# One step of attention, another order of TensorE's score halves, logits and mixes

## The chip, the core and the metric

The kernel runs on one core of a Trainium2 chip. The metric is the device time of the whole program in microseconds (us): 3871.87 is the median of three runs of the kernel before (3871.11 to 3872.05).

TensorE (PE) does the matrix products, VectorE (DVE) and ScalarE (ACT) read its results out of PSUM, GpSimd (POOL) adds in SBUF and issues the accumulating transfers, SyncE (SP) issues the plain ones. Each engine runs its own instructions strictly in the order in which the program lists them, and waits on semaphores that the others raise.

## What is computed

Cross-attention with grouped queries: 4 batches, 1024 queries, 1601 keys, 32 heads of 32, 8 key/value heads (4 query heads share one), then an output projection, a residual and a layer norm, all in float32.

```python
q = hidden_state @ Wq + bq;  k = encoder_hidden_state @ Wk + bk;  v = encoder_hidden_state @ Wv + bv
scores = jnp.einsum('bkgld,bksd->bkgls', q, k) * scale + encoder_attention_mask[:, :, None, :, :]
attn = jax.nn.softmax(scores, axis=-1)
out = jnp.einsum('bkgls,bksd->bkgld', attn, v)
x = out.transpose(0, 3, 1, 2, 4).reshape(b, l, H) @ Wo + bo + hidden_state
return (x - mean(x)) * rsqrt(var(x) + EPS) * gamma + beta
```

The mask of these inputs is zero everywhere. The kernel tests that on the chip and takes a branch without mask work.

## The kernel before

Three stages follow each other. `project` makes q, k and v and writes them to DRAM. `attend` does the attention, and it is all that the change touches. `output` does the projection and the norm.

`attend` runs 64 steps: a step is 512 queries of one batch with one key/value head and its 4 query heads. Steps are written out in groups of four (`QUAD`). Work of one step, by the letters of the string `ORDER` (line 475):

- **S**, a score half (line 821): two matmuls over half of the 1601 keys into one of the two `score` buffers, for 128 queries of one head. VectorE then takes the maximum over them (line 972). There are 32 in a step, for the step after this one. After the last of a step, VectorE joins the halves to `row_max` (line 976).
- **T**, once: the row maxima of the next step are transposed into a `logit` bank (line 852). ScalarE and VectorE split them into two parts `parts_t` (lines 1036, 984), and SyncE copies these as two more rows under that step's queries (`shift`, line 632), so that the logits come out with the maximum taken off.
- **L**, a logit tile (line 866): 128 keys by 512 queries of one head, one matmul into one of three `logit` banks. ScalarE takes the exponential into `weights` (line 1030). There are 52 in a step: 13 key tiles (0 to 12) of 4 heads.
- **M**, a mix (line 876, from `mix`): weights times values for one key tile. Four heads side by side, each 32 columns of the array. It needs the four exponentials of its tile. There are 13 in a step; the first of a step's string is tile 12 of the step before (`FIRST_MIX = 1`).
- **P**, once: the sums over the keys (`denominators`, line 876 too) of the step before, from `sum_pool`.

The order of TensorE's work is this string, read from left to right in every step; ScalarE follows the same string, and VectorE follows the sequence of the S. Between the letters stand the waits. An S waits until VectorE has read the score half two before it. L, T and P take the three `logit` banks in turn, so each waits for the reader of the third before it. A mix waits for its exponentials.

GpSimd adds the weights of 9 of the 13 tiles into `sum_pool` by 8 adds (line 736). The other four (2, 5, 8, 11) are added by accumulating transfers that it issues (three at line 747; `merge` at line 754 adds their sum to `sum_pool` after the first add of the next step, once the third has landed). ScalarE may overwrite a weights buffer only when its mix and its add are done: the exponentials of tile 4, the 17th to 20th L of a step, take the buffer of tile 12 of the step before, whose add is GpSimd's eighth.

SyncE's own order within a step: the queries and keys of a later step (`load_step`, lines 603 and 606, once the 52nd L of the step is done), their values (lines 610 and 611, once the step's last mix is done), the store of the mixed rows, the store of the sums (line 645, after P and its copy), and then the shift rows (line 632).

Of the kernel before, what the change touches and what calls it, by code (L numbers as in the profile page):

```python
# [53 lines left out]
def xattn_program(nc, x, ctx_kv, mask, wq, bq, wk, bk, wv, bv, wo, bo, gamma, beta, out):  # L54
    x_flat = x.rearrange("b l h -> (b l) h")
    ctx_flat = ctx_kv.rearrange("b s h -> (b s) h")
    mask_flat = mask.rearrange("b o l s -> (b o l) s")
    out_flat = out.rearrange("b l h -> (b l) h")

    q_dram = nc.dram_tensor("q_parts", [NLQ, KVH, 2, P, LQ], F32, kind="Internal").ap()  # L60
    k_dram = nc.dram_tensor("k_parts", [2, KV, B * S], F32, kind="Internal").ap()
    v_dram = nc.dram_tensor("v_rows", [B * S, KV], F32, kind="Internal").ap()
    a_dram = nc.dram_tensor("weighted", [NSTEP, P, LQ], F32, kind="Internal").ap()
    d_dram = nc.dram_tensor("denominators", [NSTEP, G, LQ], F32, kind="Internal").ap()
    r_dram = nc.dram_tensor("reciprocals", [NSTEP, G, LQ], F32, kind="Internal").ap()
    wo_dram = nc.dram_tensor("wo_parts", [2 * KVH, P, H], F32, kind="Internal").ap()

    with ExitStack() as whole:
        ident = whole.enter_context(nc.sbuf_tensor("ident", [P, P], F32))
        mask_size = whole.enter_context(nc.sbuf_tensor("mask_size", [P, MT], F32))  # L70
        project(nc, x_flat, ctx_flat, mask_flat, wq, bq, wk, bk, wv, bv, wo, q_dram, k_dram, v_dram, wo_dram, ident, mask_size)

        qk_store = [whole.enter_context(nc.sbuf_tensor(f"qk_store{i}", [P, G * LQ + S], F32R)) for i in range(3)]
        wo_spare = whole.enter_context(nc.sbuf_tensor("wo_spare", [P, H], F32R))
        wo_in = whole.enter_context(nc.semaphore("wo_parts_in"))
        wo_slots = [store[:, t * H:(t + 1) * H] for store in qk_store for t in range(SLOTS)] + [wo_spare[:]]
        attend(nc, mask_flat, q_dram, k_dram, v_dram, a_dram, d_dram, r_dram, wo_dram, ident, mask_size, qk_store, wo_spare, wo_in)
        output(nc, x_flat, wo_slots, wo_in, wo_dram, bo, gamma, beta, a_dram, d_dram, r_dram, out_flat)
# [384 lines left out]
def attend(nc, mask_flat, q_dram, k_dram, v_dram, a_dram, d_dram, r_dram, wo_dram, ident, mask_size, qk_store, wo_spare, wo_in):  # L463
# [8 lines left out]
    LATE = 10  # L472
    NPOOL = len(POOL) - 1

    ORDER = "LLLSLSLLSLMSLLSLMMSLLSLLSLSLLSLMMSLLSLLSLSLLSLMMSLLSLLSLSLLSLPMMLSLSLLLSLSTMMLLSLLSLSLLSLSLLSLMMSLS"
    FIRST_MIX = 1
    LO_AT = 24
    assert [ORDER.count(k) for k in "LSMTP"] == [ST * G, 2 * NROW, ST, 1, 1]
    BANKS = 3
    USES = [k for k in ORDER if k in "LTP"]  # L480
    assert len(USES) % BANKS == 0
# [40 lines left out]
    with ExitStack() as held:  # L522
# [278 lines left out]
        def _(pe):  # L801
# [105 lines left out]
            def quad_steps(quad, masked, first=False, last=False):  # L907
                for s in range(QUAD):
                    u = k = 0
                    tile = s * ST - FIRST_MIX  # L910
                    for work in ORDER:
                        if work == "L":
# [96 lines left out]
        def _(act):  # L1009
# [40 lines left out]
            def quad_steps(quad, first=False, last=False):  # L1050
                for s in range(QUAD):
                    u = mixes = 0
                    for work in ORDER:
                        if work == "L":
# [259 lines left out]
```

## Time and profile before

| | |
|---|---|
| time, median of three runs | 3871.87 us |
| the profiled execution: its own time | 3873.77 us |
| its span | 3872.1 us |
| TensorE busy | 3769.2 us (97%) |
| TensorE weight loads busy | 2379.7 us (61%) |
| VectorE busy | 2496.9 us (64%) |
| ScalarE busy | 2033.2 us (53%) |
| GpSimd busy | 2895.5 us (75%) |
| attention, from the first P to the 62nd | 900.09 to 3415.97 us |
| TensorE's granted clock from 900 to 3416 us | 1.00 |

Times count from the start of the span. In the busy time of TensorE the matmuls overlap each other: the next one starts before the last has ended. So the distance between two starts tells more than the durations. A mix appears as 8 matmuls, so "x16" is two mixes and "x12" is one and a half, where a window cuts; a score half appears as "x2", a logit tile as "x1".

### The profile page before, as it was taken

Reading aid. Unit: us, or ns where it says so; the run is one execution under the profiler, and the core shown is the slowest. Engines: PE = TensorE matmul, PEld = TensorE weight load, DVE = VectorE, ACT = ScalarE, POOL = GpSimd, SP = SyncE. Lnnn points to the kernel's source line nnn. Section 1 sums busy time; section 2 is a strip of 40 time slices with the busy share of each in tenths; the row PEclk is TensorE's granted clock in tenths of the full one; section 3 lists DMA queues with packets and bytes.
Section 4 is the critical chain, followed back from the end, with each engine's and each line's share of the span. In section 5 each row is a group of like instructions: output and inputs, shape, how many; then the busy total and the mean of one; then the engine's idle time right before and its main releaser. Section 6 shows DMA issues by size and latency. Waiting matters only on the chain. (4 is left out here: it accounts for less than half of the span.)

```text
span 3872.1 us, 55400 instructions
## 1 busy us (share of the span) xinstructions
PE 3769.2 (97%) x20306; PEld 2379.7 (61%) x20306; DVE 2496.9 (64%) x2904; ACT 2033.2 (53%) x3854; POOL 2895.5 (75%) x1104
## 2 busy tenths in 40 slices
PE   8999999789999999999999999999999999988998
PEld 7998888545555555555555555555555555536886
DVE  3334444477777777777777777777777777725665
ACT  2222112126666666666666666676666666661110
POOL 1111111139999999999999999999999999984555
PEclk9999999869999999999999999999999999998999
DMA  5344555647667667667667667677677677667664
GB/s 176 136 150 177 201 198 200 246 85 152 146 146 155 145 145 158 143 145 159 146 144 158 145 146 158 141 151 155 139 155 151 141 155 149 146 150 220 194 191 125
DMA packets 294100, 611.94 MB, mean 158 GB/s; under 512 B 131696, under 2 KB 168688, under 8 KB 261360
## 3 DMA queue, kind: packets, MB, share of 16 engines
q0 software_dynamic: 58080, 337.15, 38.7%
q1 hardware_dynamic: 232528, 265.54, 25.7%
q10 hardware_dynamic: 3264, 6.29, 0.5%
q8 instruction: 134, 2.20, 0.2%
q14 instruction: 94, 0.77, 0.1%
HBM read 244.50 MB, written 96.99 MB: 88 GB/s over the span
## 5 line engine op out<-in xcount | busy, mean ns | idle before, releaser
L972 DVE TENSOR_REDUCE half_max<-score 128x1 f32<-128x800 f32 (+1 forms) x2048 | 1893.7, 986 | 714.2 <-PE score L821 710.2
L1030 ACT ACTIVATE weights<-logit 128x512 f32<-128x512 f32 (+1 forms) x3328 | 1732.4, 602 | 791.6 <-PE logit L866 765.6
L736 POOL TENSOR_TENSOR sum_pool<-sum_pool,weights 128x2048 f32<-128x2048 f32 x446 | 2125.6, 4766 | 29.6 <-ACT weights L1030 2.5
L821 PE MATMUL score<-qk_store 96*128 96x400 f32 (+1 forms) x4096 | 1212.2, 378 | 14.9 <-DMA qk_store<-k_parts 10.4
L866 PE MATMUL logit<-qk_store 98*128 98x512 f32 (+1 forms) x3328 | 1199.5, 417 | 2.3 <-ACT weights L1030 2.2
L821 PEld LDWEIGHTS score<-qk_store 96*128 96x128 f32 x4096 | 688.5, 191 | 552.6 <-DVE half_max L972 397.5
L876 PE MATMUL mixed<-weights,v_sb 128*32 128x512 f32 x6656 | 807.8, 599 | 0.7 <-ACT weights L1030 0.7
L866 PEld LDWEIGHTS logit<-qk_store 98*128 98x128 f32 (+1 forms) x3328 | 607.8, 185 | 264.0 <-ACT weights L1030 135.1
L876 PEld LDWEIGHTS mixed<-weights,v_sb 128*32 128x32 f32 x6656 | 177.0, 109 | 393.2 <-ACT weights L1030 218.6
L736 POOL TENSOR_TENSOR sum_pool<-weights 128x2048 f32<-128x2048 f32 x64 | 313.7, 4901 | 63.6 <-ACT weights L1030 63.6
L450 POOL DMA_DIRECT2D q_parts<-o_hi x64 | 34.5, 540 | 306.1 <-DVE o_lo L412 149.3
L1192 PE MATMUL acc<-qk_store,a_hi 128*128 128x512 f32 x576 | 187.0, 397 | 25.1 <-DVE a_lo L1227 25.1
L347 ACT ACTIVATE o_hi<-summed,bq_scaled 128x512 fp32r<-128x512 f32 x64 | 44.1, 689 | 304.0 <-PE summed L259 274.3
L325 ACT CAST t_hi<-turned 128x512 fp32r<-128x512 f32 x168 | 95.6, 585 | 141.8 <-PE turned L254 141.8
L407 DVE TENSOR_SCALAR full<-summed,bq_scaled 128x512 f32<-128x512 f32 x64 | 48.0, 751 | 188.5 <-ACT o_hi L347 188.5
L747 POOL DMA_DIRECT2D weights<-weights x191 | 165.9, 868 | 0.0
L1281 POOL TENSOR_TENSOR total<-total,beta_row 128x1024 f32<-128x1024 f32 x32 | 100.4, 3139 | 76.3 <-DVE total L1248 76.3
L1274 POOL TENSOR_TENSOR total<-total,bo_row 128x1024 f32<-128x1024 f32 x32 | 89.6, 2806 | 85.4 <-DMA total<-in_x 85.2
L456 POOL DMA_DIRECT2D v_rows<-v_store x52 | 28.1, 540 | 160.1 <-DMA v_rows<-v_store 101.5
L1192 PEld LDWEIGHTS acc<-qk_store,a_hi 128*128 128x128 f32 x576 | 109.4, 190 | 52.6 <-issue 26.0
L372 DVE TENSOR_TENSOR t_lo<-turned,t_hi 128x512 fp32r<-128x512 f32 x168 | 113.1, 685 | 42.6 <-ACT t_hi L325 42.4
L259 PE MATMUL summed<-t_hi,wq_hi 128*128 128x512 f32 x512 | 134.6, 404 | 0.0
(87 smaller groups left out, 2772.4 us busy)
## 6 DMA issues: line engine op xcount, KB each, us to landing
weights<-weights POOLq DMA_DIRECT2D x191, 1024.0 KB, 7.3
sum_pool<-weights POOLq DMA_DIRECT2D x63, 1024.0 KB, 7.0
qk_store<-q_parts SPq DMA_DIRECT2D x192, 256.0 KB, 3.9
qk_store<-k_parts SPq DMA_DIRECT2D x192, 200.1 KB, 5.4
rows<-in_ctx SPq DMA_DIRECT2D x26, 1024.0 KB, 5.1
landing<-in_mask_Bx1xSxS_ff SPq DMA_DIRECT2D x32, 800.5 KB, 5.5
rows<-in_x SPq DMA_DIRECT2D x16, 1024.0 KB, 5.1
q_parts<-o_hi POOLq DMA_DIRECT2D x64, 256.0 KB, 2.4
```

The costliest lines, as they stand in the source:

```text
L259: last = nc.tensor.matmul(acc, lhs, rhs, start=(n == 0), stop=(n == len(pairs) - 1))
L325: nc.scalar.copy(t_hi[par][:, t, :], turned[t % 2][:]).then_inc(hi_done, 1)
L372: nc.vector.tensor_tensor(t_lo[par][:, t, :], turned[t % 2][:], t_hi[par][:, t, :].bitcast(F32), ALU.subtract).then_inc(lo_done, 1)
L736: nc.gpsimd.tensor_tensor(sum_pool[s % 2][0:w], first[0:w], weights[buffer(s, st)][0:w], ALU.add).then_inc(pool_added, 1)
L747: pool.dma_start(weights[buffer(s, REST[0])][:], weights[buffer(s, st)][:], accum_op=ALU.add).then_inc(rest_added, 16)
L821: last = nc.tensor.matmul(score[j][:, c, 0:w], q_sb[buf][0:STACK, h, lt * P:(lt + 1) * P], k_sb[buf][0:STACK, start:start + w], start=True ...
L866: last = nc.tensor.matmul(bank[0:w, :], k_sb[s][:, keys], q_sb[s][:, h, :], start=True, stop=not masked, skip_group_check=masked)
L876: last = nc.tensor.matmul(out[h * HD:(h + 1) * HD, :], lhs, rhs[0:w, h, :], start=start, stop=stop)
L972: nc.vector.tensor_reduce(half_max[m // NROW % 2][:, k % G, k // G, j:j + 1], score[j][:, :, 0:HALVES[j][2]], mybir.AxisListType.XY, ALU.m ...
L1030: nc.scalar.activation(weights[buffer(s, st)][0:w, h, :], logit[u % BANKS][0:w, :], ACT.Exp).then_inc(exp_done, 1)
L1192: last = nc.tensor.matmul(acc[j * NT + t][:, n, :], a[:, k, cols], w[k][:, out_cols], start=(k == 0 and m == 0), stop=(k == KVH - 1 and m ...
L1281: nc.gpsimd.tensor_tensor(total[r][:], total[r][:], beta_row[:], ALU.add).then_inc(final, 1)
```

## The change

One string is another. It has the same letters in the same numbers, 52 L, 32 S, 13 M, one T, one P, and all else is as it was.

```diff
@@ -472,7 +472,7 @@
     LATE = 10
     NPOOL = len(POOL) - 1
 
-    ORDER = "LLLSLSLLSLMSLLSLMMSLLSLLSLSLLSLMMSLLSLLSLSLLSLMMSLLSLLSLSLLSLPMMLSLSLLLSLSTMMLLSLLSLSLLSLSLLSLMMSLS"
+    ORDER = "LLMSLLSLLSLLSLSLLSLLSLLSLLSLLSLSLLLSLSMMMMSLLSLLSLLSLSLLSLLSLLSLMLTSLSMMMSLSMMPLSLLSLLSLLSLLSLMMSLS"
     FIRST_MIX = 1
     LO_AT = 24
```

A visit is a run of M and P without anything else between. Before there are seven in a step: M, MM, MM, MM, PMM, MM, MM. Now there are six: M, MMMM, M, MMM, MMP, MM.

TensorE, before, inside the branch without mask, from one pair of mixes to the P (score is an S, logit an L, the second operand `weights,v_sb` a mix):

```order
L876 MATMUL mixed<-weights,v_sb 32x512 x8
L821 MATMUL score<-qk_store 128x402 x2
L866 MATMUL logit<-qk_store 128x512 x2
L821 MATMUL score<-qk_store 128x400 x2
L866 MATMUL logit<-qk_store 128x512 x2
L821 MATMUL score<-qk_store 128x402 x2
L866 MATMUL logit<-qk_store 128x512
L821 MATMUL score<-qk_store 128x400 x2
L866 MATMUL logit<-qk_store 128x512 x2
L821 MATMUL score<-qk_store 128x402 x2
L866 MATMUL logit<-qk_store 128x512
L876 MATMUL logit<-sum_pool,ones 32x512 x4
```

The pair of mixes is 8 instructions here. Five S and eight L stand between two visits, and an L is the last of them.

TensorE now, the end of the longest run and what follows it:

```order
L866 MATMUL logit<-qk_store 128x512 x2
L821 MATMUL score<-qk_store 128x402 x2
L866 MATMUL logit<-qk_store 128x512
L821 MATMUL score<-qk_store 128x400 x2
L866 MATMUL logit<-qk_store 128x512 x3
L821 MATMUL score<-qk_store 128x402 x2
L866 MATMUL logit<-qk_store 128x512
L821 MATMUL score<-qk_store 128x400 x2
L876 MATMUL mixed<-weights,v_sb 32x512 x16
L821 MATMUL score<-qk_store 128x402 x2
```

Four mixes (16 instructions) stand together, and the last thing before them is an S. The run before them holds 13 S and 22 L.

TensorE now, from the third visit to the P:

```order
L876 MATMUL mixed<-weights,v_sb 32x512 x4
L866 MATMUL logit<-qk_store 128x512
L852 MATMUL logit<-ident,row_max 16x128
L821 MATMUL score<-qk_store 128x402 x2
L866 MATMUL logit<-qk_store 128x512
L821 MATMUL score<-qk_store 128x400 x2
L876 MATMUL mixed<-weights,v_sb 32x512 x12
L821 MATMUL score<-qk_store 128x402 x2
L866 MATMUL logit<-qk_store 128x512
L821 MATMUL score<-qk_store 128x400 x2
L876 MATMUL mixed<-weights,v_sb 32x512 x8
L876 MATMUL logit<-sum_pool,ones 32x512 x4
```

The transpose T stood after the P before (35th L, then 41st); now it comes first, after 39 L, and the P comes after 41. ScalarE's copies of both move with them.

## Rows read from the trace of the kernel before

**Rows 1.** The page's groups: busy time, mean ns, idle before, releaser

```profile
L972 DVE TENSOR_REDUCE half_max<-score 128x1 f32<-128x800 f32 (+1 forms) x2048 | 1893.7, 986 | 714.2 <-PE score L821 710.2
L1030 ACT ACTIVATE weights<-logit 128x512 f32<-128x512 f32 (+1 forms) x3328 | 1732.4, 602 | 791.6 <-PE logit L866 765.6
```

**Rows 2.** TensorE in order of time, one step: start, duration, instruction, count

```profile
1989.08 0.98 PE L866 MATMUL logit<-qk_store 98*128 98x512 f32 x3
...
1992.32 1.07 PE L876 MATMUL mixed<-weights,v_sb 65*32 65x512 f32 x8
1993.32 0.63 PE L821 MATMUL score<-qk_store 96*128 96x402 f32 x2
...
1994.96 1.92 PE L876 MATMUL mixed<-weights,v_sb 128*32 128x512 f32 x16
...
2007.29 1.92 PE L876 MATMUL mixed<-weights,v_sb 128*32 128x512 f32 x16
2009.15 0.64 PE L821 MATMUL score<-qk_store 96*128 96x402 f32 x2
2009.63 0.62 PE L866 MATMUL logit<-qk_store 98*128 98x512 f32 x2
2010.09 0.53 PE L821 MATMUL score<-qk_store 96*128 96x400 f32 x2
2010.45 0.76 PE L866 MATMUL logit<-qk_store 98*128 98x512 f32 x2
...
2013.16 0.39 PE L866 MATMUL logit<-qk_store 98*128 98x512 f32 x1
2013.48 1.06 PE L876 MATMUL logit<-sum_pool,ones 128*32 128x512 f32 x8
...
2019.71 1.92 PE L876 MATMUL mixed<-weights,v_sb 128*32 128x512 f32 x16
...
2027.38 1.92 PE L876 MATMUL mixed<-weights,v_sb 128*32 128x512 f32 x16
...
2033.54 1.06 PE L876 MATMUL mixed<-weights,v_sb 65*32 65x512 f32 x8
```

**Rows 3.** The same view, the 62nd P

```profile
3415.97 1.06 PE L876 MATMUL logit<-sum_pool,ones 128*32 128x512 f32 x8
```

**Rows 4.** VectorE in order of time; in brackets its idle time before

```profile
2003.65 4.59 DVE L972 TENSOR_REDUCE half_max<-score 128x1 f32<-128x800 f32 x5 [1.57 <-PE score L821]
```

**Rows 5.** ScalarE in order of time, in that burst and in the last step

```profile
2003.88 4.21 ACT L1030 ACTIVATE weights<-logit 128x512 f32<-128x512 f32 x8 [1.97 <-PE logit L866]
...
3439.18 4.03 ACT L1030 ACTIVATE weights<-logit 128x512 f32<-128x512 f32 x8 [1.08 <-PE logit L866]
```

**Rows 6.** GpSimd in order of time, one cycle of it

```profile
1992.67 4.89 POOL L736 TENSOR_TENSOR sum_pool<-sum_pool,weights 65x2048 f32<-65x2048 f32 x1
...
2002.55 0.87 POOL L754 DMA_DIRECT2D sum_pool<-weights  x1 [0.44 <-POOL sum_pool L736]
...
2033.05 0.87 POOL L747 DMA_DIRECT2D weights<-weights  x1
2033.64 4.88 POOL L736 TENSOR_TENSOR sum_pool<-sum_pool,weights 65x2048 f32<-65x2048 f32 x1
2038.16 4.91 POOL L736 TENSOR_TENSOR sum_pool<-weights 128x2048 f32<-128x2048 f32 x1
2043.33 0.87 POOL L754 DMA_DIRECT2D sum_pool<-weights  x1 [0.26 <-POOL sum_pool L736]
```

**Rows 7.** SyncE's transfers in order of time

```profile
2015.43 0.63 SPq L645 DMA_DIRECT2D denominators<-denom_sb  x1
2021.06 1.17 SPq L632 DMA_DIRECT2D qk_store<-parts_t  x2
2030.34 1.34 SPq L603 DMA_DIRECT2D qk_store<-q_parts  x3
```

**Rows 8.** From the view of the tile parts_t: landing of the shift rows' transfers

```profile
DMA to landing us min/median/max: 1.8/1.8/5.6
```

## The prediction

> **What bounds the kernel now.** First the page's groups [rows 1]: VectorE's maxima wait 710 us in all for a score, ScalarE's exponentials 766 us for a logit. Neither reader is the bound over the whole. Next, TensorE in order of time: 900.09 (first P; in the table of times) and 3415.97 [rows 3] are 61 steps apart, 41.24 us each, and the step in [rows 2] (1992.32 to 2033.54) has 41.22. TensorE never stands long, so the question is what its slots hold. From [rows 2] by distances of starts:
>
> - an S takes 0.36 (2010.09 to 2010.45), which I take as 0.365, two L 0.46 (2009.63 to 2010.09), so 0.235 each;
> - a visit with one mix occupies 1.00 (1992.32 to 1993.32), one with two 1.86 (2007.29 to 2009.15): a mix is 0.857, and leaving costs 0.115 to 0.14. The first S behind a visit takes 0.48 instead of 0.365: 0.115 more. The last L before one takes 0.32 (2013.16 to 2013.48): 0.09 more. A visit thus costs 0.32 beside its mixes.
>
> A step's slots are 52 x 0.235 + 32 x 0.365 + 14 x 0.857 + 0.20 for T = 36.1, and seven visits add 2.3. The remaining 2.8 of 41.24 are waits inside the runs between visits. [Rows 4] show whose: in a run VectorE takes five halves in 4.59 back to back, each complete after 0.986 [rows 1], so one per (4.59 - 0.99) / 4 = 0.90 (0.901 unrounded); then it idles 1.57 while TensorE mixes. An S needs the half two before it read, so within a run TensorE goes at VectorE's pace, and in a visit VectorE starves, because only what stands in two score buffers is left for it. ScalarE's pace is read from the last step, which has no S and where it is the limit: eight exponentials in 4.03 [rows 5], one complete after 0.60 [rows 1], so one per (4.03 - 0.60) / 7 = 0.49.
>
> **The change part by part.** Nothing is computed more or less; only runs and visits are cut differently. I write a step as its mixes, 14 x 0.857 = 12.0, plus the runs between visits.
>
> Before, from [rows 2], each run being a visit's start less the start and mixes of the visit before: 1.78 (2 S, 3 L), two of 4.45, 4.48 behind 2009.00 (each 5 S, 8 L), 3.66 (4 S, 6 L, T; 2016.05 to 2019.71), 5.96 (6 S, 11 L; 2021.42 to 2027.38), 4.45 (5 S, 8 L). Together 29.2; with the mixes 41.2, as measured.
>
> The rule for a run: it begins with 0.23 of leaving and refilling; VectorE begins 0.20 behind the first S's slot; after that S number n can start only 0.06 after half n-2 has been read, plus 0.115 because its weights were not loaded ahead; then its own slot, a trailing L, and 0.09 for entering. For n = 5: 0.23 + 0.365 + 0.20 + 2 x 0.90 + 0.99 + 0.17 + 0.365 + 0.235 + 0.09 = 4.45, which is the measured run.
>
> Now, by the same rule, run by run:
> - 13 S and 22 L, ending in an S: 0.23 + 0.565 + 10 x 0.901 + 1.155 + 0.365 + 0.09 = 11.42 (1.155 is 0.985 + 0.17). ScalarE has 22 x 0.49 = 10.8 beside it and little room where three L stand together; I add 0.14: 11.56.
> - 8 S, 14 L: 0.23 + 0.565 + 5 x 0.901 + 1.155 + 0.60 + 0.09 = 7.15; with 0.07 for ScalarE 7.22.
> - L T S L S: slots and a visit's cost, 1.70. S L S: 1.30.
> - 5 S, 10 L behind the P: here ScalarE is slower, 10 x 0.49 against 5 x 0.90: 4.91.
> - S L S and the two L of the next step: 1.76, as the 1.78 before.
> Sum 28.45, and with the mixes 40.45. The same walk gives 41.15 for the step before, 0.09 under the trace, so I put 40.54. Where the 0.7 comes from: 0.3 is the visit less; 0.4 is that three runs now end in an S directly before the visit, so VectorE has up to two halves to read when a visit begins, and starves less often. The longest visit costs it nothing more per mix.
>
> The Trainium skill, TensorEngine Tiling (Array Packing), Key Properties, says that a change of tiling mode drains TensorE. Counted by that rule alone the change is worth one drain in a step, 0.3 x 62 = 20 us; [rows 4] say that more than half of the gain is VectorE's, which that rule doesn't hold.
>
> What the trace doesn't show is a visit entered directly from an S (three times now). The nearest rows are an L before it (0.09 more than its slot) and the next score behind an S without any cost; I take 0.09, with 0 and 0.19 as ends: 3 x 62 x -0.09 to 3 x 62 x +0.10, or -17 to +19 us.
>
> **GpSimd.** Its cycle from one merge's issue to the next is 2043.33 - 2002.55 = 40.78 [rows 6], nearly the step. Without a wait it would be 2038.16 - 2002.55 = 35.61 and one add of 4.52 (2038.16 - 2033.64), together 40.13. The rest is the wait of the merge for the third accumulating transfer, issued 2033.05, merge 2043.33: 10.3 us for one that otherwise lands in 7. It collides with the query and key loads, which SyncE issues at 2030.34 [rows 7], behind the 52nd L. These are tied to TensorE's step, and so GpSimd follows it. A step of 40.54 is 0.4 above GpSimd's 40.13, so it can follow, with less room. One place gets tight: the 17th L now ends 8.9 us behind the step's first instead of 11.3 (slots and runs as above), and its exponential overwrites the buffer whose add is GpSimd's last. That add starts at 1992.67 and ends at 1997.56, 8.5 behind the step's first L (1989.08). In a step shorter by 0.6 it ends at 9.1, and the exponential would start at 9.1. That is no room on average; where GpSimd is a few tenths late, ScalarE waits. I add 0.06 a step, with 0 and 0.5 as ends.
>
> The Trainium skill, DMA: Bandwidth & Descriptors, Queues, rings and completion order, says that each DMA engine takes turns between the queues it has work for. The 10.3 against 7 us agrees. By it the value loads, which now start earlier since the first mix stands behind two L, leave the third transfer alone sooner, and the added term would be 0.
>
> **Shift rows.** P moves to 31.8 behind the first L (24.4 before: 2013.48 - 1989.08). The store of the sums starts 1.95 behind it (2015.43) and holds SyncE 0.63; the shift rows are queued behind: they start at 34.4, take 1.17 to issue and land 1.8 later [rows 8], at 37.4. The next step's first L is at 40.5. Even 4 us of landing still fits; in one step of four a load of sums stands between and takes this room. Cost 0, at worst 0.1 a step.
>
> **Sum.** (41.24 - 40.60) x 62 steps = 40 us. The profiled execution had 3873.77; it becomes 3834, and the median, 1.9 below it, 3832.
>
> **The rivals.**
> 1. GpSimd doesn't follow. If the third transfer keeps landing as late, at the cycles of 40.8 to 41.2 that [rows 6] show, the 17th exponential waits for it in each step, and the step is 40.95 to 41.2: 3854 to 3869, 3860 as its middle. For it: almost no room, and a cycle that now is longer than my step. Against it: the transfer would be issued later behind the loads, where it collides less.
> 2. ScalarE paces the long runs: slower. In a burst its eight exponentials take 4.21 [rows 5], one per 0.516. If that were its pace, and not TensorE's, the three logit banks would hold back every L of the runs with two L per S. My walk with 0.52 gives 41.13 for the new step, no gain, and with 0.53 41.44 (+0.3, 3890); from 0.525 an exponential on it is slower. Against it: 0.49 in the last step.
> 3. Only the visit counts: VectorE's starvation is the same because halves are read at the same total rate. Then 0.32 x 62 = 20 us: 3852. Against it: the run rule gives the measured 4.45.
> 4. Nothing of GpSimd shows and entering from an S is free: 40.2 to 40.4, 3808 to 3820.
>
> **How the numbers follow.** Forecast, a step of 40.45 to 40.75: 0.52. Rival 1: 0.17; rival 2: 0.08; rival 3: 0.10; rival 4: 0.13. The range goes from 3812 (part of rival 4) to 3866 (most of rival 1) and leaves rival 2. About 0.2% (8 us) is what a measurement of this kernel can tell from no change: faster is everything but a part of rival 1 and rival 2, 0.85; same 0.08; slower 0.07.
>
> **What would show it.** Right: P to P 40.6; six visits; the run of 13 S some 11.5 us with VectorE's halves 0.90 apart; ScalarE's wait for GpSimd's adds small and at tile 4. Wrong: a wait of ScalarE for `sum_pool` in each step and cycles of POOL and TensorE equal (rival 1); exponentials back to back through the long run with VectorE waiting there (rival 2); the long run at 12 us or more; a wait of the first L for the shift rows.

## The result, and the profile after

| us | before | after |
|---|---|---|
| median | 3871.96 | 3903.39 |
| lowest to highest, 4 runs each | 3871.11 to 3873.01 | 3898.64 to 3908.74 |
| profiled execution, its span | 3873.77, 3872.1 | 3908.74, 3907.1 |
| a step of attention, mean | 41.24 | 41.78 |

The ratio is 1.0082 (95%: 1.0067 to 1.0097): slower by 0.8%, where 3832 was forecast, with faster at 0.85. The forecast is wrong in its sign. The mean of after is that of 60 steps between P's (905.03 to 3411.78), where [rows 3] gave 41.24 before.

The page's groups of after, which answer to [rows 1]: busy time, mean ns, idle before, releaser.

```profile
L972 DVE TENSOR_REDUCE half_max<-score 128x1 f32<-128x800 f32 (+1 forms) x2048 | 1924.2, 987 | 723.9 <-PE score L821 719.7
...
L1030 ACT ACTIVATE weights<-logit 128x512 f32<-128x512 f32 (+1 forms) x3328 | 1705.7, 615 | 737.7 <-PE logit L866 705.0
L866 PE MATMUL logit<-qk_store 98*128 98x512 f32 (+1 forms) x3328 | 1237.6, 431 | 31.7 <-DMA qk_store<-parts_t 23.3
```

VectorE and ScalarE are no more the bound than they were. New in the last row is the wait: TensorE's logits wait for the shift rows. First, though, what the order does where nothing disturbs it: TensorE at one single mix of after, at the visit of four behind it and at the next single mix (start, duration, instruction, count); they answer to [rows 2].

```profile
1208.53 1.07 PE L876 MATMUL mixed<-weights,v_sb 65*32 65x512 f32 x8
...
1220.96 3.64 PE L876 MATMUL mixed<-weights,v_sb 128*32 128x512 f32 x32
...
1249.05 1.06 PE L876 MATMUL mixed<-weights,v_sb 65*32 65x512 f32 x8
```

From 1208.53 to 1249.05 are 40.52: the forecast of 40.54 for this walk is met. So the loss is in other steps, and it begins at two waits. Here is GpSimd in order of time in after, three merges and the add before two of them, with the idle time before each in brackets; they answer to [rows 6].

```profile
926.60 0.87 POOL L754 DMA_DIRECT2D sum_pool<-weights  x1 [1.97 <-DMA weights<-weights]
...
962.22 4.92 POOL L736 TENSOR_TENSOR sum_pool<-weights 128x2048 f32<-128x2048 f32 x1
968.77 0.87 POOL L754 DMA_DIRECT2D sum_pool<-weights  x1 [1.64 <-DMA weights<-weights]
...
1004.37 4.92 POOL L736 TENSOR_TENSOR sum_pool<-weights 128x2048 f32<-128x2048 f32 x1
1011.10 0.87 POOL L754 DMA_DIRECT2D sum_pool<-weights  x1 [1.81 <-DMA weights<-weights]
```

From one merge to the next are 42.17 and 42.33 (the next two, at 1052.82 and 1094.47, follow after 41.72 and 41.65). GpSimd works without a pause from a merge to the first add (35.62, as in [rows 6]), then adds for 4.5 to 4.9, and then stands 1.2 to 2.0 in these until the third accumulating transfer has landed. It cannot keep a step of 40.54, falls behind by a microsecond or so in each, and this comes out in one of two places. The first is the 17th exponential, ScalarE in order of time:

```profile
1038.63 7.06 ACT L1030 ACTIVATE weights<-logit 128x512 f32<-128x512 f32 x14 [0.18 <-PE logit L866]
1047.18 3.55 ACT L1030 ACTIVATE weights<-logit 128x512 f32<-128x512 f32 x7 [1.49 <-POOL sum_pool L736]
```

GpSimd's eighth add began at 1042.18 and took 4.91 in this step, so ScalarE waited until 1047.18, and TensorE's next logit 1.22. The second place is the shift rows. In another step, SyncE's shift rows, GpSimd's second accumulating transfer, and TensorE:

```profile
2245.28 1.93 SPq L632 DMA_DIRECT2D qk_store<-parts_t  x2
```

```profile
2243.92 0.87 POOL L747 DMA_DIRECT2D weights<-weights  x1
```

```profile
2222.80 3.64 PE L876 MATMUL mixed<-weights,v_sb 128*32 128x512 f32 x32
...
2252.59 0.73 PE L866 MATMUL logit<-qk_store 98*128 98x512 f32 x2 [2.09 <-DMA qk_store<-parts_t]
...
2254.35 1.04 PE L821 MATMUL score<-qk_store 96*128 96x400 f32 x2
2255.18 1.05 PE L866 MATMUL logit<-qk_store 98*128 98x512 f32 x2
...
2268.63 3.64 PE L876 MATMUL mixed<-weights,v_sb 128*32 128x512 f32 x32
```

GpSimd is late, so its second transfer (2243.92) starts beside the shift rows (2245.28), and they land some 7 us after their issue. The load of sums, which one step in four has, stands ahead of them here too (2244.82), as the prediction said that it might: 10 of the 23 waits for the shift rows, and 12.2 of their 23.3 us, fall in such steps. TensorE stands 2.09. After that its slots are twice as long: an S takes 0.83 (2254.35 to 2255.18) instead of 0.365. The windows of after show why (busy us of each engine, granted clock, DMA share, GB/s):

```profile
2209.00:2250.00 41.00, 40.29 (x228) 22.41 (x229) 29.66 (x35) 27.37 (x55) 40.47 (x13) 1.00 0.73 152
...
2252.00:2259.00 7.00, 6.41 (x22) 4.58 (x23) 2.53 (x3) 3.95 (x8) 7.00 (x3) 0.65 0.97 224
2259.00:2260.00 1.00, 1.00 (x4) 0.91 (x3) 0.47 (x2) 0.97 (x2) 0.48 (x1) 0.50 1.13 231
```

Behind the stand the granted clock goes to 0.50, the 1.2 GHz level. From one visit of four to the next (2222.80 to 2268.63) are 45.83, 5.3 more than an undisturbed step, and only 2.1 of it is the stand. Before, the clock is 1.00 throughout attention; in after it is 0.97 to 0.99 in every window of 400. The loss is not spread evenly. From P to P, 21 of the 60 steps take less than 40.6, and twelve take over 44. These twelve hold 54 of the 74 us that the 60 lie above 40.55, and they are the twelve in which the clock fell.

The sum: 41.78 - 40.54 over 62 steps is 77 us. From the views of waits, of before first and then of after (us in total, times, longest):

```profile
PE logit L866 <- ACT weights L1030: 2.2, 9, 0.3
PE score L821 <- DVE half_max L972: 1.3, 6, 0.5
...
POOL sum_pool L754 <- DMA weights<-weights: 34.5, 31, 2.1
```

```profile
PE logit L866 <- DMA qk_store<-parts_t: 23.3, 23, 2.4
PE logit L866 <- ACT weights L1030: 7.9, 9, 1.7
PE score L821 <- DVE half_max L972: 5.0, 20, 0.5
...
POOL sum_pool L754 <- DMA weights<-weights: 61.4, 42, 2.8
```

The last row of each is GpSimd's merge. TensorE's waits for the shift rows and for ScalarE grew by 23.3 + 5.7 = 29. The clock that is missing from 1.00 in the windows from 900 to 3400 is worth about 41 us (each is rounded to a hundredth, so give or take 12); the trace's own record of the clock has twelve stretches at 0.50, 75 us together, which is 37.5 us of lost work. A third term is in neither: one step in four is 0.4 longer even undisturbed, 6 us, and e8 shows what it is. What TensorE's small waits for VectorE grew by (from 1.3 to 5.0) is a part of this one, since it lies in those steps alone. 29, 37.5 and 6 are 72 of the 77; the rest stays open. How the clock's share can be that large is tested in e10 below.

### The profile page after: what moved, and what is told of

It reads as the page before. It is cut to its first block and busy times, and to the rows that moved or that the text cites. A ratio compares the mean times of both kernels' runs of the same rounds, so it can differ in the third digit from the quotient of the medians.

```text
span 3907.1 us, 55401 instructions
## 1 busy us (share of the span) xinstructions
PE 3774.8 (97%) x20306; PEld 2404.8 (62%) x20306; DVE 2514.7 (64%) x2904; ACT 2000.3 (51%) x3854; POOL 2896.4 (74%) x1104
## 5 line engine op out<-in xcount | busy, mean ns | idle before, releaser
L972 DVE TENSOR_REDUCE half_max<-score 128x1 f32<-128x800 f32 (+1 forms) x2048 | 1924.2, 987 | 723.9 <-PE score L821 719.7
L1030 ACT ACTIVATE weights<-logit 128x512 f32<-128x512 f32 (+1 forms) x3328 | 1705.7, 615 | 737.7 <-PE logit L866 705.0
L866 PE MATMUL logit<-qk_store 98*128 98x512 f32 (+1 forms) x3328 | 1237.6, 431 | 31.7 <-DMA qk_store<-parts_t 23.3
L821 PE MATMUL score<-qk_store 96*128 96x400 f32 (+1 forms) x4096 | 1196.5, 374 | 16.9 <-DMA qk_store<-k_parts 10.3
L821 PEld LDWEIGHTS score<-qk_store 96*128 96x128 f32 x4096 | 721.9, 195 | 422.5 <-issue 173.3
L866 PEld LDWEIGHTS logit<-qk_store 98*128 98x128 f32 (+1 forms) x3328 | 622.5, 188 | 387.8 <-ACT weights L1030 272.9
L450 POOL DMA_DIRECT2D q_parts<-o_hi x64 | 34.5, 540 | 305.2 <-DVE o_lo L412 153.1
```

Of the source, the lines that this page charges most:

```text
L821: last = nc.tensor.matmul(score[j][:, c, 0:w], q_sb[buf][0:STACK, h, lt * P:(lt + 1) * P], k_sb[buf][0:STACK, start:start + w], start=True ...
L866: last = nc.tensor.matmul(bank[0:w, :], k_sb[s][:, keys], q_sb[s][:, h, :], start=True, stop=not masked, skip_group_check=masked)
L972: nc.vector.tensor_reduce(half_max[m // NROW % 2][:, k % G, k // G, j:j + 1], score[j][:, :, 0:HALVES[j][2]], mybir.AxisListType.XY, ALU.m ...
L1030: nc.scalar.activation(weights[buffer(s, st)][0:w, h, :], logit[u % BANKS][0:w, :], ACT.Exp).then_inc(exp_done, 1)
```

## The experiments

Times of before, measured beside them: 3869.37 (e1 to e4), 3871.82 (e5 to e8), 3872.05 (e9, e10), 3871.75 (e11, e12).

**e1: shift rows earlier.** In SyncE's order, ahead of the store of the sums.

```diff
+                        if not (final and n == KVH - 1):
+                            shift(step + 1, (n + 1) % QB)
                         if not (first and lq == 0 and n == 0):
                             store_sums(step - 1)
...
-                        if not (final and n == KVH - 1):
-                            shift(step + 1, (n + 1) % QB)
```

> The changed kernel with one edit: in SyncE's order the shift rows of the next step stand ahead of the store of the sums (and of the load of sums), so they no longer wait for P and its copy. Theory 1 (the shift rows are late because they are queued behind P, and run beside the second accumulating transfer; each late landing stops TensorE 1 to 2.3 us and halves its granted clock for some us after): no wait of a logit for parts_t, most steps at the undisturbed 40.54 us, 3830 to 3850 us. Theory 2 (GpSimd's cycle is the bound, 41.7 us because its merge waits 1.6 us for the third accumulating transfer; the shift waits are only where TensorE is held): the waits move to the exponentials of tile 4, which wait for GpSimd's last add, the mean step stays at 41.5 to 41.8, 3885 to 3905 us. Both together would give something between, near 3870.

Measured: 3897.55, ratio 1.0068 (1.0051 to 1.0085). TensorE's waits for the shift rows are gone from the view of waits, and only 6 us of after's time went with them. The other wait has taken their place:

```profile
ACT weights L1030 <- POOL sum_pool L736: 65.4, 48, 3.4
...
PE logit L866 <- ACT weights L1030: 35.7, 43, 2.1
```

After had 24.7 us in 12 waits in the first row. The shift rows are where the loss came out and not its cause. The clock behaves as in after, but not behind each stand: of the 14 stands of over 1 us, eight are followed by the 1.2 GHz level and six are not (1.46 at 1423.00 is the longest of these, with 1.00 from 1423 to 1429).

**e2: the merge one add later.**

```diff
                     add(quad, s, n)
-                    if n == 0 and not first:
+                    if n == 1 and not first:
                         merge(quad * QUAD + (s - 1), s - 1)
```

> The changed kernel with one edit: GpSimd issues the merge behind its second add of the next step instead of behind its first, so the third accumulating transfer has 14.7 us to land instead of 9.6. Theory 2 (GpSimd's cycle with its wait for that transfer is the bound): the wait goes, the cycle can be 40.13 us, GpSimd keeps up with TensorE's 40.54, the second accumulating transfer stops drifting into the shift rows, 3830 to 3840 us. Theory 1 (the shift rows behind P alone): P stays where it is, TensorE still waits for the shift rows in some 25 steps, 3880 us or more.

Measured: 3836.96, ratio 0.9910 (0.9894 to 0.9927). The merge waits for nothing any more. GpSimd from one merge to the next, in order of time:

```profile
2190.68 0.87 POOL L754 DMA_DIRECT2D sum_pool<-weights  x1
...
2216.47 0.87 POOL L747 DMA_DIRECT2D weights<-weights  x1
...
2226.70 4.57 POOL L736 TENSOR_TENSOR sum_pool<-sum_pool,weights 128x2048 f32<-128x2048 f32 x1
2231.22 0.85 POOL L754 DMA_DIRECT2D sum_pool<-weights  x1
```

2231.22 - 2190.68 = 40.54: GpSimd keeps TensorE's step. The third transfer has the time until 2231.22, 14.8 us, instead of the 10 that the old place gave it. The shift rows are not touched by this edit; they land after 2.7 us in the median (3.9 in after), no logit waits for them, and the granted clock is 1.00 in every window of attention. One wait was the cause of both others and of the clock. What remains of the step's excess is the 0.4 in one step of four.

**e3: both edits.**

> The changed kernel with the edits of e1 and e2 together. Either theory: step 40.54 us nearly throughout, 3828 to 3835 us; if both waits were only symptoms of something else (TensorE's granted clock falling for the long visits by themselves), the time stays near 3900 and the clock near 0.97.

Measured: 3835.49, ratio 0.9908 (0.9891 to 0.9924), 1.5 under e2: the shift rows' place adds nothing that can be told apart once the merge is late. They now land after 6.2 us in the median, beside the second transfer, and no logit waits for them: what counts is when they must be there.

**e4: small transfers.** In after, the three accumulating transfers of a step carry 16 of 2048 columns.

```diff
-                pool.dma_start(weights[buffer(s, REST[0])][:], weights[buffer(s, st)][:], accum_op=ALU.add).then_inc(rest_added, 16)
+                pool.dma_start(weights[buffer(s, REST[0])][:, 0:1, 0:16], weights[buffer(s, st)][:, 0:1, 0:16], accum_op=ALU.add).then_inc(rest_added, 16)
```

> The changed kernel with the three accumulating transfers of a step cut to 16 of 2048 columns (the weights of tiles 5, 8 and 11 are left out of the denominators except in these columns); the merge keeps its size. It takes away the 7 us transfers that load the DMA engines and that the merge waits for. Theories 1 and 2 alike: shift rows land in 1.8 us, no wait of the merge, GpSimd ahead, step 40.54 us, 3828 to 3835 us. If TensorE lost its time to the order itself (entering visits from a score, the long visits, the clock), it stays near 3900.

Measured: 3835.95, ratio 0.9909 (0.9893 to 0.9926). With the traffic gone and the merge in its old place, the time is e2's. It is the duration of the transfer and not the place of an instruction that was too long.

**e5: P earlier**, in the third visit (`...SLPMLTSLSMMMSLSMMLS...`), so that the sums are stored sooner.

> The changed kernel with one edit of the string: the P moves from the fifth visit (MMP) to the third (PM), 8 us earlier, so the store of the sums no longer holds the shift rows; the number of visits and the runs stay. Theory 2 (the merge's wait for the third accumulating transfer makes GpSimd's cycle 41.5 us, and that is the bound): as with the shift rows first, waits at tile 4 and a mean step near 41.6, 3885 to 3905 us. Theory 1 (P's place): 3835 us.

Measured: 3900.41, ratio 1.0070 (1.0053 to 1.0086). As e1: no wait for the shift rows, but ScalarE waits 48.8 us in 35 places for GpSimd and the merge 71.2 in 53.

**e6: before, with the small transfers of e4.**

> The kernel before with the three accumulating transfers cut to 16 of 2048 columns (the weights of tiles 5, 8 and 11 are left out of the denominators but for these columns). If the kernel before is bound by TensorE with its two readers and not by GpSimd, the step stays at 41.24 us and the time at 3865 to 3872. If its 41.24 was GpSimd's cycle with its wait, it falls below 41, 3850 us or less.

Measured: 3868.90, ratio 0.9992 (0.9983 to 1.0002). The step stays at 41.24, so before loses nothing to the third transfer. In before the merge waits too (34.5 us in 31 places), but a step of 41.24 leaves GpSimd's cycle just room. The new string took that room away.

**e7: loads later.** In after, `load_step` stands at the end of SyncE's turn.

> The changed kernel with one edit in SyncE's order: the loads of queries, keys and values for a later step stand at the end of a step's list, behind the shift rows, instead of at its start. They then run beside the second accumulating transfer and no longer beside the third, for which the merge waits. If the collision with these loads makes the third transfer slow (10.6 instead of 7 us), the merge's wait goes and the step is near 40.6, 3833 to 3845 us, unless the loads now slow the shift rows. If the third transfer is slow by itself, nothing changes, about 3900 us.

Measured: 3904.36, ratio 1.0079 (1.0062 to 1.0096). It decides nothing: SyncE's turn ends so early that the loads (1826.90 in one step) still start ahead of the third transfer (1830.79), which lands after 10.6 us in the median as before the edit (10.7).

**e8: e3, and VectorE's `invert` five halves later**, since e2 and e3 still had one step of four 0.4 longer than the others.

```diff
-                        if s == 2 and k == 8 and not first:
+                        if s == 2 and k == 13 and not first:
                             invert(quad - 1)
```

> The changed kernel with the shift rows first, the merge behind the second add, and VectorE's reciprocal of the denominators (once in four steps) moved from before its 9th score half to before its 14th, the first behind the visit of four mixes, where VectorE idles. In the kernel with the first two edits every fourth step is 40.95 instead of 40.55 us. If the reciprocal in the long run is the cause, all steps are 40.55: 15 x 0.4 = 6 us less, 3829 us; if it is the load of sums or something else of that step, 3835 us as it was.

Measured: 3829.83, ratio 0.9891 (0.9875 to 0.9908), the fastest kernel of the study: 1.1% under before and 1.9% under after. Its visits, TensorE in order of time:

```profile
1209.36 3.64 PE L876 MATMUL mixed<-weights,v_sb 128*32 128x512 f32 x32
...
1220.16 1.06 PE L876 MATMUL mixed<-weights,v_sb 128*32 128x512 f32 x8
...
1222.67 2.78 PE L876 MATMUL mixed<-weights,v_sb 128*32 128x512 f32 x24
...
1226.55 1.92 PE L876 MATMUL mixed<-weights,v_sb 128*32 128x512 f32 x16
1228.29 1.04 PE L876 MATMUL logit<-sum_pool,ones 128*32 128x512 f32 x8
...
1233.99 1.92 PE L876 MATMUL mixed<-weights,v_sb 128*32 128x512 f32 x16
...
1237.49 1.06 PE L876 MATMUL mixed<-weights,v_sb 65*32 65x512 f32 x8
```

The next visit of four began at 1249.91, 40.55 after 1209.36. Less 0.857 a mix, the runs are 7.37, 1.65, 1.31, 4.87, 1.79 and 11.56; the prediction had 7.22, 1.70, 1.30, 4.91, 1.76 and 11.56. From P to P every step is 40.5 to 40.8, so the reciprocal in the long run was the 0.4: a term of 0.1 a step, 6 us, that after has, before has not and the prediction left out.

**e9: loads in the middle.** In after, `load_step` waits for 28 logits more, so the loads start some 15 us into the step and not beside the third transfer (`more` is 28 at its two calls for later steps and 0 elsewhere).

```diff
-                sp.wait_ge(logit_done, step * (ST * G) + ST * G)
+                sp.wait_ge(logit_done, step * (ST * G) + ST * G + more)
```

> The changed kernel with one edit: the loads of queries, keys and values for a later step wait for 28 more logits, so they start some 15 us into the step, between GpSimd's merge and its first accumulating transfer, and not beside the third one. (In e7 they moved by only some 4 us and still ran beside it.) If the collision is what makes the third transfer land after 10.6 us and not after 7, it lands after 7 to 8.5, the merge doesn't wait, the step is 40.6 and the time 3833 to 3842 us. If the transfer is slow for another reason, about 3900 us.

Measured: 3922.61, ratio 1.0137 (1.0120 to 1.0154), the slowest but one, where 3833 to 3842 was expected if the collision was the cause. SyncE and GpSimd in one step:

```profile
1811.76 2.51 SPq L606 DMA_DIRECT2D qk_store<-k_parts  x3
```

```profile
1811.55 0.87 POOL L747 DMA_DIRECT2D weights<-weights  x1
...
1824.58 0.87 POOL L747 DMA_DIRECT2D weights<-weights  x1 [2.82 <-issue]
...
1834.70 0.88 POOL L747 DMA_DIRECT2D weights<-weights  x1
...
1844.42 1.19 POOL L754 DMA_DIRECT2D sum_pool<-weights  x1
```

The third transfer (1834.70) is now alone, and the merge follows the add at once; over the whole it waits 1.2 us in one place. The third transfers land after 7.0 us in the median, where after has 10.7. So it was the loads that made the third transfer slow. But now the first one has them beside it (1811.55; 10.8 in the median instead of 7.0), the second may only start when it has landed, and GpSimd stands 2.82 there: 79 us in all at line 747. The wait has moved along a chain of three transfers, and the expectation failed by that. The shift rows come late again too (38.2 us in 41 waits). The Trainium skill, DMA: Bandwidth & Descriptors, Queues, rings and completion order, says that DMA engines take turns between the queues that they have work for. This trace agrees: the transfer beside the loads takes 10.8 and the one without them 7.0, so this move only chose which one is slowed.

**e10: one stand by design.** e8, in which in one step of four the shift rows wait for the step's last logit.

```diff
                         if not (final and n == KVH - 1):
+                            if n % QUAD == 0:
+                                sp.wait_ge(logit_done, step * (ST * G) + ST * G + LOGITS0)
+                                sp.sem_inc(sync_seen, 1)
                             shift(step + 1, (n + 1) % QB)
```

> The kernel of e8 (no waits, every step 40.55 us) in which SyncE issues the shift rows of one step in four only after that step's 52nd logit, so TensorE stands still once in four steps, some 2.5 to 3 us, 16 times. If a stand costs its own length, the time rises by 16 x 2.8 = 45 us, to 3875. If TensorE's granted clock falls to 1.2 GHz after it, as the long steps of the changed kernel suggest (3 us beyond the wait), by 16 x 5.8 = 93 us, to 3920, and the steps with the stand and the one behind it show it.

Measured: 3972.15, ratio 1.0258 (1.0241 to 1.0275), 142.3 over e8, or 8.9 for each of 16 stands; both expectations (3875 and 3920) had the stands too short. The view of waits, and TensorE at one of them (lines are three later than in the others):

```profile
PE logit L869 <- DMA qk_store<-parts_t: 85.5, 16, 6.5
```

```profile
2071.73 0.54 PE L824 MATMUL score<-qk_store 96*128 96x402 f32 x2
2077.39 1.22 PE L869 MATMUL logit<-qk_store 98*128 98x512 f32 x2 [5.13 <-DMA qk_store<-parts_t]
...
2086.24 0.58 PE L824 MATMUL score<-qk_store 96*128 96x400 f32 x2
```

```profile
2077.00:2079.00 2.00, 1.61 (x6) 0.70 (x10) 0.00 (x0) 0.69 (x2) 0.57 (x1) 0.50 1.07 133
2079.00:2086.00 7.00, 7.00 (x23) 5.00 (x16) 2.98 (x3) 4.20 (x8) 0.00 (x0) 0.50 0.98 214
```

The stands are 85.5 / 16 = 5.3 each; 3.5 remain. From the first logit behind the stand to 2086.24 are 8.85 at the 1.2 GHz level; in e8 the same letters take 5.07 (1236.93 to 1242.00), 3.8 less. So a stand costs its length and some 3.5 us of slow slots more, in a kernel where nothing else is late. This bears out the clock's share in after, 37.5 us in twelve falls or 3.1 each. What sets whether a short stand is followed by one was not tried; e1 has stands of 1.1 to 1.5 with and without.

**e11: an L instead of an S ahead of three visits.** e8, with `LS` exchanged to `SL` ahead of MMMM, MMM and MMP.

> The kernel with the later merge, the earlier shift rows and the shifted inversion (e8: 3829.83, a step of 40.55), and in the string the three visits that are entered from an S are entered from an L instead (LS before MMMM, MMM and MMP becomes SL). Run rule of the prediction: only the run of 13 S is at VectorE's pace, it gets a trailing logit slot, 0.235, behind its last S; the short runs hold slots only and stay. Step 40.79, 3829.8 + 62 x 0.235 = 3844. The sentence of the prediction that 0.4 of the gain is these three S before a visit: 40.95, 3855. Rival that the place of the S counts for nothing and only the number of visits does: 3830.

Measured: 3843.53, ratio 0.9928 (0.9915 to 0.9942), 13.7 over e8 or 0.22 a step. The run of 13 S is 11.82 (1158.96 to 1171.64, less a mix) instead of 11.56; the short runs are unchanged within 0.02. This is the run rule's number (3844).

**e12: the visit of four split.** e8, with an S and an L between two pairs.

```diff
-...LLLSLSMMMMSLLSLL...
+...LLLSLSMMSLMMLSLL...
```

> The same kernel (e8), and the visit of four mixes split into two of two with one S and one L between, both taken from the front of the run that follows: seven visits in a step as before the change, the same letters. By a price for each visit beside its mixes (0.32, a drain for each change of the tiling): step 40.87, 3849. By the run rule: the new short run is slots and a visit's cost, 0.365 + 0.235 + 0.32 = 0.92, and the run behind it, at VectorE's pace, has one S less, 0.90 less: step 40.57, 3831, no change, since a visit only costs where VectorE does not set the pace. Rival that longer visits starve VectorE and the split feeds it: below 3826.

Measured: 3839.73, ratio 0.9916 (0.9903 to 0.9930), 9.9 over e8, or 0.16 a step; from P to P it is 40.68 against 40.55, so 0.13. TensorE in order of time:

```profile
1130.40 1.93 PE L876 MATMUL mixed<-weights,v_sb 128*32 128x512 f32 x16
1132.25 0.63 PE L821 MATMUL score<-qk_store 96*128 96x402 f32 x2
...
1133.04 1.92 PE L876 MATMUL mixed<-weights,v_sb 128*32 128x512 f32 x16
1134.90 0.50 PE L866 MATMUL logit<-qk_store 98*128 98x512 f32 x1
...
1141.31 1.06 PE L876 MATMUL mixed<-weights,v_sb 128*32 128x512 f32 x8
```

The new run is 0.93 as both theories had it, and the run behind it 6.56 where e8 has 7.37. A visit more thus costs 0.32 in its own slots. The run behind it is 0.81 shorter, and the S and the L that left it are 0.60 of slots: 0.2 of the 0.32 comes back. That VectorE has a half less to read there fits, but isn't shown apart. Neither theory has the sum: a drain for each visit gave 3849, the run rule 3831. The rule had 0.90 for the 0.81. It left out that the run now begins with an L, its first S 0.33 later; why that costs 0.1 and not 0.33 stays open.

## Why the prediction was wrong

**What failed: "These are tied to TensorE's step, and so GpSimd follows it", and "it can follow".** I took GpSimd's cycle without the merge's wait, 40.13, as what it can do, and let the wait shrink by as much as the step did. But the loads are issued behind TensorE's 52nd L and the third transfer behind GpSimd's own seventh add, and wherever it was issued in after, the loads lay beside it for long enough: it lands after 10.7 us in the median (9.0 to 12.3), where before had 10.0 (8.6 to 11.6). The warning was there in two forms. [Rows 6] show two merges that waited 0.44 and 0.26, the smallest part of it: over all 63 it was 34.5 us in 31 places, which the view of waits would have told. And the one cycle in [rows 6], 40.78, was already over my step of 40.6; over all of before the cycles go from 40.2 to 43.0, with TensorE's 41.25 as their mean. With the waits of after they are 41.7 to 42.3 in the rows shown. e2 and e4 show that this step was the cause: they take the wait away in two ways and give 3837 and 3836.

**The price of being late, 0.06 a step with 0.5 as its end.** It is 1.2 a step: 0.1 is ScalarE's wait at tile 4, the one place that was priced, 0.4 the shift rows (0, at worst 0.1, in the prediction), 0.6 the clock (in no term) and 0.1 VectorE's reciprocal (in no term). Two things were outside of the range. One: "even 4 us fits" for the shift rows. [Rows 8] had 1.8 as the median, but 5.6 as the longest, and the question to ask was what would lie beside them at their new place. It is GpSimd's second transfer, 1.4 us ahead of them in the step shown, and in one step of four the load of sums too; they take up to 7.0. Two: behind twelve of the 13 stands of 1.0 to 2.4 us in after the clock is at the 1.2 GHz level for some microseconds, which costs more than the stand (e10). No stand of that size was in the attention of before.

**Rival 1** was the mechanism (0.17), with a step of 40.95 to 41.2 and so still not slower. It held GpSimd's old cycle as a ceiling, and had the 17th exponential wait in each step; in after that wait is there 12 times, and most of the loss came out at the shift rows. After is at 41.78. Without the clock's 37.5 us it would be 41.2 (an estimate from the sum above), the upper end of this rival.

**What held.** The run rule: six runs within 0.15 of the forecast, step 40.55 against 40.54. Entering a visit from an S costs 0.10 (1249.44 to 1249.91, less a slot), taken as 0.09. Rival 2 is out: the run of 13 S is 11.56 with 22 exponentials in it. One of its signs came all the same: in e8 ScalarE's 22 there follow each other in 11.13 us (from 1198.83) and VectorE's 13 halves in 12.11 (from 1198.60), so 0.93 apart and not 0.90. Both readers are near their pace in that run, and the 0.14 added for ScalarE was a guess that came out. Rival 4 too: nothing is below 3829.8. With GpSimd's wait removed the time is 3836.96 (e2), 5 over the forecast of 3832, about what the reciprocal costs (6); 3829.83 is a kernel with two edits more.

**What held only in part.** "0.4 is that three runs now end in an S": e11 gives 0.22 for all three, and all of it in the one run where VectorE sets the pace. "0.3 is the visit less" and rival 3: e12 puts 0.13 to 0.16 on it. The Trainium skill, TensorEngine Tiling (Array Packing), Key Properties, has a drain at each change of tiling mode. The slots agree (1.85 from 1130.40 to 1132.25 for two mixes of 0.857), and in e12 more than half of a visit's 0.32 is given back in the run behind it, where VectorE sets the pace. What makes the remaining 0.3 of the 0.7 was not separated.

## What to carry to other kernels

Before a loop is made shorter, take the cycle of every engine that waits for a transfer in it, with the wait, over many turns, and treat it as fixed until the trace shows what the transfer collides with. If that cycle comes close to the loop (here 40.78 against 40.6), move the consumer of the transfer away from it first (one instruction here, worth 66 us), and only then tighten the order. And price a new stand of TensorE at more than its length: where the clock falls behind it, some 3 us more in this kernel.

## What was not expected of the hardware

- An accumulating transfer of 1 MB inside SBUF lands in 6.9 us at the least and in up to 12.3 beside loads from DRAM (view of line 747 in after).
- The shift rows, two small transfers, land in 1.8 us or in up to 7.9 (e9), by what is beside them.
- Behind stands of 1.2 and 2.1 us TensorE ran at a granted clock of 0.50 for a few microseconds, behind 5.1 us for nine, and each time it came back to 1.00 while the engine worked on. Stands of like length differ: behind 1.31 us in e1 (1212.90) the clock is 0.52 from 1214 to 1221, behind 1.46 us (1423.00) it stays at 1.00.
